# A four-layer transformer stack on one NeuronCore: later turns of normed rows, a spread of halves in four pieces, and later loads of three batches' tokens

## The reference

```python
# 1. causal attention, 16 heads of 8, with a relative bias per distance
logits = where(j <= i, (q @ k.T + take_along_axis(q @ rel_key.T, clip(j - i + 255, 0, 255))) * scale, -inf)
out = softmax(logits) @ v @ Wo + bo
# 2. gated FFN with integer weights / 127, hidden size 384
out = (silu(x @ w_gate.T) * (x @ w_up.T)) @ w_down.T
# 3. quaternion attention, 16 heads of 8, not causal: q and k are quaternion-linear and normed
q = quat_norm(quat_linear(x, qW, qb)); k = quat_norm(quat_linear(x, kW, kb)); v = quat_linear(x, vW, vb)
out = quat_linear(softmax(q @ k.T * scale + 0.1 * mean(sin(J))) @ v, oW, ob)
# 4. mixture of 8 experts, the best two of each token, hidden size 512, gelu
out = sum over the two best of p_e * (gelu(x @ w1_e + b1_e) @ w2_e + b2_e)
```

## Time and profile before

| | |
|---|---|
| median of 3 runs | 871.47 us (870.83 to 872.36) |
| time of the profiled execution | 872.1 us |
| its span, first to last instruction | 869.9 us |
| PE busy (matmuls) | 736.0 us, 85% of the span |
| PE weight loads (beside matmuls) | 522.1 us, 60% |
| ACT busy | 501.3 us, 58% |
| DVE busy | 419.1 us, 48% |
| POOL busy | 180.4 us, 21% |
| mean granted TensorE clock | 0.947 of full speed |
| rounds 1, 2, 3, 4, 5 begin on PE at about | 120, 227, 374, 518, 642 us |

### The profile page before, as it was taken

The page is one execution under the profiler, slowest core; times in us unless marked ns, Lnnn a source line. Parts: engine busy times, 40 slices in busy tenths (PEclk is TensorE's granted clock), DMA queues, the critical chain, the costliest instruction groups (busy, mean ns, idle before and its releaser), DMA issues. The chain is left out here.

```text
span 869.9 us, 21028 instructions
## 1 busy us (share of the span) xinstructions
PE 736.0 (85%) x8160; PEld 522.1 (60%) x8160; DVE 419.1 (48%) x1389; ACT 501.3 (58%) x1030; POOL 180.4 (21%) x307
## 2 busy tenths in 40 slices
PE   4779997989779999888989987887786878789994
PEld 3668775768545667665555753455553656467763
DVE  3355426664253464225353566473866646531236
ACT  3456564586557586866658765558454556543231
POOL 7101010000100000010100005132315287036230
PEclk9999998999889999999999999999887999989997
DMA  4610400002400000511000412000511021101010
GB/s 113 204 15 3 152 7 5 5 2 64 126 4 14 17 2 15 149 29 17 4 15 1 127 46 72 19 22 22 165 46 43 26 80 37 33 26 50 19 40 24
DMA packets 72358, 40.43 MB, mean 46 GB/s; under 512 B 42726, under 2 KB 62140, under 8 KB 72132
## 3 DMA queue, kind: packets, MB, share of 16 engines
q1 hardware_dynamic: 70468, 35.81, 15.1%
q0 software_dynamic: 1536, 3.15, 1.2%
q10 hardware_dynamic: 256, 0.13, 0.1%
HBM read 20.98 MB, written 17.96 MB: 45 GB/s over the span
## 5 line engine op out<-in xcount | busy, mean ns | idle before, releaser
L954 ACT ACTIVATE late<-ps,j_bias 128x512 f32<-128x512 f32 x256 | 173.9, 695 | 136.3 <-PE ps L1768 135.4
L1220 DVE TENSOR_REDUCE neg_max<-ps 128x2 f32<-128x32 f32 (+31 forms) x128 | 90.5, 707 | 188.3 <-PE ps L1612 179.7
L1768 PE MATMUL ps<-q_heads,k_parts 128*128 128x512 f32 x256 | 131.6, 531 | 20.8 <-ACT late L954 17.2
L794 ACT ACTIVATE probsT<-ps 128x128 f32<-128x128 f32 (+3 forms) x271 | 102.8, 429 | 76.7 <-PE ps L1627 50.0
L880 ACT ACTIVATE probs<-ps,neg_max 128x16 f32<-128x16 f32 (+31 forms) x256 | 110.5, 494 | 16.7 <-DVE neg_max L1220 16.3
L1627 PE MATMUL ps<-ident,probs 128*128 128x128 f32 x640 | 97.1, 283 | 7.5 <-ACT probs L880 7.5
L664 POOL TENSOR_TENSOR q_wide<-qT,eighth_mask 128x1024 f32<-128x1024 f32 x16 | 31.3, 1954 | 303.2 <-PE ps L1612 175.9
L1627 PEld LDWEIGHTS ps<-ident,probs 128*128 128x128 f32 x640 | 76.8, 144 | 26.7 <-ACT probs L880 10.7
L1768 PEld LDWEIGHTS ps<-q_heads,k_parts 128*128 128x128 f32 x256 | 48.5, 197 | 68.9 <-ACT late L954 46.7
L1783 PE MATMUL ps<-late,v_two 128*9 128x512 f32 x512 | 71.3, 630 | 10.9 <-DVE late L1206 8.7
L1605 PE MATMUL ps<-kT_two,q_wide 64*64 64x262 f32 (+16 forms) x1024 | 74.8, 357 | 4.4 <-ACT probsT L794 2.7
(11 more groups left out here) (271 smaller groups left out, 1166.3 us busy)
## 6 DMA issues: line engine op xcount, KB each, us to landing
k_parts<-k_half SPq DMA_DIRECT2D x16, 256.0 KB, 3.1
q_parts<-q_half SPq DMA_DIRECT2D x16, 256.0 KB, 3.9
k_parts<-k_parts SPq DMA_DIRECT2D x16, 256.0 KB, 3.3
q_heads<-q_parts SPq DMA_DIRECT2D x64, 64.0 KB, 2.2
x_by_expert<-q_heads SPq DMA_DIRECT2D x3, 960.0 KB, 7.7
probsT<-x_by_expert SPq DMA_DIRECT2D x45, 64.0 KB, 1.9
y_by_expert<-probsT SPq DMA_DIRECT2D x45, 64.0 KB, 1.5
q_rel<-q_by_token SPq DMA_DIRECT2D x128, 8.0 KB, 2.4
```

What stands on the lines that cost most here:

```text
L794: return nc.scalar.activation(o, i, ACT.Copy)
L954: nc.scalar.activation(head_probs[:, i % SLOTS, :], ps[:, banks[i % len(banks)], :], ACT.Exp, bias=j_bias[:]).then_inc(e2_ready.sem, 1)
L1220: nc.vector.tensor_reduce(neg_max[:, n % 4, :], ps[:, k:k + OCT, 0:QS * (n + 1)], axis=AXX, op=ALU.max, negate=True).then_inc(max_ready.se ...
L1768: mm(ps[:, banks[i % R], :], k_parts[:, hg, kc * P:(kc + 1) * P], q_heads[:, hg % 2, g, :], start=True, stop=True).then_inc(s2_ready.sem, 1)
```

## The change

It edits four things in the plan and SP's program; no operation is added or taken away.

1. In rounds with attention, pieces 5 and 6 of F (piece 5 is the turn of the FFN's normed rows) stand in slots 14 and 15 for 11 and 12, plus `late`, which is 2 from round 2 on. In round 4 the pieces from 5 on begin in slot 19 for 16, and the last 12 in slot 40 for 39; the second turn, piece 25, stands first among these.
2. `spread` has two more yields: the stores, the first loads back, the next loads, the rest. S stands in slots 52, 55, 58 and 63 (in round 4 in 53, 56, 59 and 63), for 52 and 63.
3. For the experts: the first five pieces of N of batch 1 in slot 52 for 51; the tiles of batch 0 from slot 33 for 30; pieces 5 and on of N of batch 2 in slots 21 to 29 and 32 to 37, for 18 to 32.
4. The three loads of `x_all` for batches 1 to 3 stand behind the loads of w1 and w2.

```diff
--- before.py
+++ after.py
@@ -93,31 +93,33 @@
             put(r, 0, "A", a - 1, 6)
             put(r, 6, "N", q - 1, 2)
             if a < B:
-                put(r, 6 + late, "F", f, 7)
+                put(r, 6 + late, "F", f, 5)
+                put(r, 14 + late, "F", f, 2)
                 put(r, 17 + late, "F", f, 17)
                 put(r, 34 + late, "F", f, 1)
                 put(r, 38 + late, "F", f, 12)
             else:
                 put(r, 8, "F", f, 5)
-                put(r, 16, "F", f, 20)
-                put(r, 39, "F", f, 12)
+                put(r, 19, "F", f, 20)
+                put(r, 40, "F", f, 12)
             if a == 0:
                 put(r, 1, "W", 0, 46)
             if a + 1 < B:
                 put(r, 41, "H", a + 1, 2)
                 put(r, 47, "H", a + 1, 10)
                 put(r, 52, "R", a + 1, 1)
-            put(r, 52, "S", f, 1)
-            put(r, SL - 1, "S", f, 1)
+            for slot in (52, 55, 58, SL - 1) if a < B else (53, 56, 59, SL - 1):
+                put(r, slot, "S", f, 1)
             if q - 1 == 0:
                 put(r, 52, "N", 0, 20)
             if q - 1 == 1:
-                put(r, 51, "N", 1, 5)
+                put(r, 52, "N", 1, 5)
                 put(r, 59, "N", 1, 15)
-                put(r, 30, "X", 0, NX, 2)
+                put(r, 33, "X", 0, NX, 2)
             if q - 1 == 2:
                 put(r, 10, "N", 2, 5)
-                put(r, 18, "N", 2, 15)
+                put(r, 21, "N", 2, 9)
+                put(r, 32, "N", 2, 6)
                 put(r, 17, "X", 1, NX, 2)
                 put(r, 33, "C", 0, 4, 3)
                 put(r, 50, "C", 0, 4)
@@ -466,8 +468,6 @@
             for m, w in enumerate(QBIAS):
                 sp.dma_start(qbias_in[:, m, :, :], w.rearrange("(a w) o -> a w o", a=1)).then_inc(ld_rows, 16)
             sp.dma_start(q_bias_rep[:], bq.rearrange("(a e) -> a e", a=1).broadcast_to([P, P])).then_inc(ld_bias, 16)
-            for b in range(1, B):
-                sp.dma_start(x_all[:, b, :, :], X[b].rearrange("(t p) e -> p t e", p=P)).then_inc(ld_x, 16)
             sp.dma_start(wi_in[:, 0, :].rearrange("p (f d) -> p f d", f=FT),
                          w_gate.rearrange("(f p) d -> p f d", p=P)).then_inc(ld_ffn, 16)
             sp.dma_start(wi_in[:, 1, :].rearrange("p (f d) -> p f d", f=FT),
@@ -515,6 +515,8 @@
             def weights(b):
                 sp.dma_start(w1_in, w1.rearrange("(m p) e d -> p m e d", p=P)).then_inc(ld_experts, 16)
                 sp.dma_start(w2_in[:], w2).then_inc(ld_experts, 16)
+                for b in range(1, B):
+                    sp.dma_start(x_all[:, b, :, :], X[b].rearrange("(t p) e -> p t e", p=P)).then_inc(ld_x, 16)
                 yield
                 yield
                 for m, w in enumerate(MATS):
@@ -544,10 +546,12 @@
                 sp.wait_ge(q_half_ready.sem, q_half_ready.at(b, 1))
                 for c in range(4):
                     sp.dma_start(q_dram[b][:, c, :, :], q_half[:, c % 2, :].bitcast(f32)).then_inc(q_out.sem, 16)
+                yield
                 sp.wait_ge(k_out.sem, k_out.at(b + 1, 0))
                 sp.wait_ge(q_out.sem, q_out.at(b + 1, 0))
                 spread_k(b, 0)
                 spread_q(b, 0)
+                yield
                 spread_k(b, 1)
                 spread_k(b, 2)
                 yield
```

## The result

The changed kernel's median is 880.69 us (878.00 to 883.54, 4 runs) against 871.51 (870.83 to 872.36, 4 runs): a ratio of 1.0105, interval 1.0072 to 1.0139. The profiled execution took 878.0 us, 5.9 more than that of before.

The account below looks back on a forecast made before the run. TensorE was taken to bound the kernel, busy 736.0 of 869.9 us, SP's queue the start. Terms -4.5 + 0.8 + 4.0 + 1.2 + 2.7 + 3.4 = +7.6 us: 872.1 to 864.5, less 0.6 gives 864; range 855 to 871.

Parts of the forecast that it names:

- H: What becomes tighter, with round 4's second turn, the spread's loads back and extra tile issues: 0, at worst -1 us.
- E: Round 4's turn, a wait of 3.23 us: quaternion steps fill it, DVE's `late` copy comes earlier; +2.7 us, ends 1.5 and 5.
- F: Round 4's tile load, a 4.68 us wait: it goes out before SP's wait for stores; +3.4 us, ends 2.1 and 7.
- A: The start: token loads behind w2 delay eight `q_rel` issues and `w_quat` in SP's queue; -4.5 us, ends 1.5 and 8.4.
- upper end of 8.4: Loss at the start if the eight `q_rel` issues cannot overtake the tokens: 5.6 + 2.8 us; forecast sum then 868.4.
- B: Round 1's turn, a wait of 5.14 us: attention there hangs on DVE, so only +0.8 us, ends 0.3 and 1.6.
- C: Round 2's turn: the 3.64 us wait goes, with a little of the half-clock stretch behind it; +4.0 us, ends 2 and 6.
- the 7.0 that the working put beside it: Round 2's gain by the skill's cold-clock rule: 3.4 us from the slow stretch plus the wait; forecast sum then 861.5.
- D: Round 3's turn: its wait of 1.23 us goes, no slow stretch counted; +1.2 us, ends 0.5 and 2.7.
- G: Round 5's turn, a 4.21 us wait: PE then waits for DVE's copy behind the same chain; 0, ends 0 and 2.
- signs named as "right": Trace signs: turn waits gone in rounds 2 to 4, clock near 1.00, `late` wait in round 5, earlier tile load in 4.
- the one on the slower side: Start: tokens keep eight `q_rel` issues at 1.70 us each, `w_quat` 13.6 us late; median 876 us, chance 0.09.

Follow-up runs that it names:

- tiles_late: Kernel before with turns of rounds 1 to 3 later, spread in four pieces, batch 0's tiles from slot 33, batch 1's first norm pieces in 52: 874.92 us, 1.0026.
- spread_and_copies: Kernel before with turns of rounds 1 to 3 later, spread in four pieces and GpSimd's copies held behind batch 2's normed rows: 863.93 us, ratio 0.9904.
- mended_all: Changed kernel with batch 2's norm line and the token loads put back and GpSimd's copies held back: 876.22 us, ratio 0.9966.
- second and third set: Two of four sets of four kernels, each set on one chip beside the kernel before, whose medians there were 879.4 and 878.9 us.
- turns_spread4: Kernel before with only the turns of rounds 1 to 3 three slots later and the spread in four pieces: 879.59 us, ratio 1.0002.

## Why the prediction was wrong

Two steps failed. The larger is H, "what becomes tighter: 0, at worst -1": it looked at the spread and at round 4 alone and had no term for round 5, where the change moves batch 2's scatters in among gathers and copies; round 5 cost 9.0 us, most of it there. The other is the sum of E and F, which gave the tiles of batch 0, three slots later, no price: +6.1 forecast, +0.2 measured. Point by point, by the working's own letters; gains are those of the profiled execution.

- **A, the start: right.** -4.5 forecast, -4.1 measured, and 0.55% by the loads alone. At the end of round 0 the four traces with the move are 3.7 to 5.2 us late, the others -2.1 to +1.1. The mechanism was a little off: the eight small issues had not to wait for w2's end; the token loads took the slow issue (9.85 us for three), and the eight 7.38. The upper end of 8.4 did not come.
- **B, round 1: near by luck.** +0.8 forecast, +0.5 measured in this trace; of the twelve others with the same edit eleven gain nothing there or lose up to 2.7, and one gains 0.4. Waits for exponentials took the place, as forecast.
- **C, round 2: right.** +4.0 forecast, +4.1 measured (2.9 to 5.1 in the thirteen traces with this edit, at most 0.8 in those without), with full clock behind it; the 7.0 that the working put beside it would have been too much.
- **D, round 3: low.** +1.2 forecast, +2.4 measured.
- **E and F, round 4: right each, wrong as a sum.** At equal counts of PE's matmuls the changed kernel is 2.9 us ahead at the round's start and 5.7 at 551: the turn gave 2.8, E's 2.7. The next tile's wait is 2.33 us and for DVE, as F had it, and the spread alone gives 2 to 3 over the round. What failed is what the working left without a price: the tiles of batch 0 from slot 33 for 30. It counted the tile's load that stands behind the spread and no other. By 610 the changed kernel is 2.6 us behind. Those tiles three slots later with F in its old place made the round 10.8 us longer in the traces (+7.9 in `tiles_late`, -2.9 in `spread_and_copies`), and all of round 4's edits but the spread cost 0.6% (`mended_all` against `spread_and_copies`).
- **G, round 5's turn: 0 forecast, and about right.** The wait changed its name as forecast, though not "at its old size": it grew from 4.21 to 8.10 us, because DVE's long operation met all of POOL's copies. That operation stood in the trace of before already (3.78 us for 128 x 4 elements), and I read the chain's end as given by PE's work, where it is given by the end of the sixteen copies. But that end hardly moved within the round. At 700 us of the kernel before, behind the stall and the turn, the changed kernel was 1.8 us ahead; at the round's start it was 1.3 ahead at equal counts of matmuls, and 3.1 by the first score. So the stall's growth cost about 1 us at most. The stall itself is a loss that both kernels have; holding the copies back removes it.
- **H: 0, at worst -1, for what becomes tighter: wrong.** It named round 4's slack, which held. The scatters that the second edit of round 5 moves (pieces 14 to 19, into slots 32 to 37, where the gathers stand at 33 and 36) had no term: some 6.8 us between the two scores of the changed kernel, 0.5% moved alone, and 1.0% with the rest of the line, of which the traces don't show all.

So the sum's 7.6 us of gain became 5.9 of loss: of the 13.5 between them 9.0 are round 5, 5.9 E and F, and A to D came out 1.4 better than forecast. All the signs named as "right" were there, the brackets gone, the clock near 1.00, `late` as the name of round 5's wait, the `q_rel` wait at 66, and the tile's load ahead of the loads back; none of them looked at the places that decided. No rival had round 5 as its place; the one on the slower side put its price at the start, where the chosen value was right.

Do the parts explain the whole? 1.010 for the line, 1.0055 for the tokens, 0.9954 and 0.9983 for the turns and about nothing for round 4 give 1.011 to 1.014, against 1.0105 (1.0072 to 1.0139) measured. Not settled is why putting the tokens back in the changed kernel left its ratio at 1.0104; that interval reaches down to 1.0063, and the median without its one late time gives 1.0062.

## What to carry to other kernels

Where a plan moves work, price each moved piece by what queues behind it on every engine, the pieces that "only shift a little" above all: tiles moved by three slots, with what moved along, cost more than the turns gained, and scatters put among copies cost half a per cent. A wait that has grown is not yet a loss: compare the same instruction on both sides of it, as the two scores of round 5 do. Look through the trace of before for small operations with durations far above their kind; such a row names the true bound of a chain, and an earlier start for it gains nothing until the other engine's burst is moved. Here one wait on GpSimd, with two of the change's parts and none of its others, gave 0.9904.

## What the runs showed of the hardware

A VectorE operation on four elements a partition can take as long as GpSimd's run of plain copies that it meets: 3.78 us in the kernel before, 5.91 in the changed one, 0.16 to 0.17 without them, and 1.96 beside one 1.95 us tensor_tensor of GpSimd in round 2. The Trainium skill ("SBUF — State Buffer", section "Who interferes with whom") has the two engines share a port that one of them holds; the traces agree, and add that the wait can span a whole run of instructions. It need not: in round 4 of the changed trace two such operations, of 0.48 and 0.52 us (619.13 and 619.65), each end with one of two back-to-back copies. Why the run of sixteen let none in until its last large copy had ended is not shown. Nor is every operation held: in the kernel before, the chain's row statistics (0.89 us at 659.84) ran beside the copies as fast as without them.

GpSimd's indirect DMAs held nothing back, with one exception: in six traces the chain's operation that began within the last scatter ahead of the copies took 0.61 to 0.65 us and ended with that scatter (656.41 + 0.63 in the changed kernel).

All eight traces of the second and third set lose 8.6 to 11.3 us in one place, whatever the kernel. In `turns_spread4` VectorE and GpSimd start again there within 20 ns, released by something that the trace calls remote:

```profile
532.16 0.69 DVE L1040 COPY outT<-ps 128x512 f32<-128x512 f32 x1 [12.02 <-remote]
532.18 0.95 POOL L721 MEMSET b_two<- 128x1024 f32 x1 [1.71 <-remote]
```

The kernel before was 0.7 to 0.8% slower in those sets too. What it is the runs don't tell.
